# First cross-attention: denominators one step later, and every stage's first weights loaded in the stage before

## The chip, the cores and the metric

The program runs on one core of a Trainium2 chip. The metric is the device time of one execution in microseconds (us), the median of the runs of a kernel. TensorE (PE in the profile) does the matmuls and transposes, VectorE (DVE), ScalarE (ACT) and GpSimd (POOL) the rest, and SyncE (SP) issues the DMAs. Each engine works through its own stream in order and waits on semaphores for the others.

## What is computed

Four blocks follow one another on x of 4 batches x 1024 tokens x 256 channels in float32. After each of them x grows by a gate (tanh) times the block's result:

```
x = x + tanh(g_xattn[0]) * L0_xattn(layernorm(x), ctx)   # 16 heads of 16, biases, 77 keys
x = x + tanh(g_ffn[0])   * L0_ffn(layernorm(x))          # ternary weights, hidden 1024, silu/gelu
x = x + tanh(g_xattn[1]) * L1_xattn(layernorm(x), ctx)   # 8 heads of 64, own layernorm, 77 keys
x = x + tanh(g_ffn[1])   * L1_ffn(layernorm(x))          # self-attention, 8 heads, 3 of 8 chosen per token
```

In L0_xattn the head outputs are sum(exp(s) v) / sum(exp(s)). The divisor, the softmax denominator, is what the first half of the change is about.

## The kernel before, in words

There are four stages, A (`first_attention`), F (`feed_forward`), C (`cross_attention`) and E (`self_attention`). Each is a block of engine streams of its own, and between two of them all engines meet at a barrier, which also waits for the last stores. Names in the trace carry the stage's letter.

**Stage A** works on 32 tiles of 128 tokens, which make 16 pairs. Every engine runs the same loop over steps `T` from -12 to 34, with `n, odd = divmod(T, 2)`. In step T (the order is that of each stream):

- PE does the scores of tile T+2, transposes the probabilities of tile T (three groups; the first comes ahead of the next item), in an odd step transposes the widened reciprocals of pair n-1 (`reciprocals(n - 1)`, L400), in an even step transposes x of pair n+2, then in an odd step projects q of pair n+2 (L385), does half of the product with V of pair n-1 (L445), and in an even step the output projection of pair n-2 (L462).
- ACT evacuates what PE transposed, in an odd step evacuates q of pair n+2 (L528), and only then takes the exponential of tile T+2 (L564).
- POOL in `T % 8 == 0` computes the inverse roots of the next batch's layer norm (`root`, 15 small instructions), in `T % 8 == 1` their offsets, then folds the exponentials of tile T+2 into eighths (`fold`, L624, L626, L630), widens the reciprocals of tile T to one per channel (`widen`, L639), in an odd step adds the bias to x (L647), in `T % 8 == 7` spreads V into blocks (`block_v`, L659), and in the steps listed in `CHUNK_STEPS` rounds a chunk of the feed-forward's weights (L652).
- DVE takes the row maxima of tile T+2 (L754), subtracts them (L769), sums the eighths of tile T+1 and inverts (`recip_sum`, L776, L777), ors a weight chunk's bits in a `CHUNK_STEPS` step (L801), does layer-norm statistics, and in even steps weighs the attention output (L762) and adds the residual (L790).

Who waits for whom around the change:

```
reciprocals(m)  (PE)   : p_wide >= 2m + 2      # both tiles' widen
fold(T)         (POOL) : a_exp >= T + 1
widen(T)        (POOL) : d_r >= T + 1
recip_sum(T)    (DVE)  : p_eighth >= T + 1
```

**Stage F** works on 8 blocks of 512 tokens. For the first block ACT copies the transposed x out of PSUM (`xt`), copies that once more rounded (`xt_part[0]`), and POOL subtracts (`xt_part[1]`). Each block is stored with one DMA.

**Stage C** begins on SP with seven loads for weights, context and layer-norm vectors, mixed with those of x. PE's first matmuls (L1143) need Wq and the layer-norm bias.

**Stage E** begins on SP with the first slices of Wq and Wk and all of Wv. ACT, in order, rounds Wq and Wk (L2247, L2248), rounds Wv (L2376), and only then copies and rounds the four quarters of the transposed x (L2268, L2254). POOL and DVE make the low parts (L2441, L2634), and PE's first projection (L2048) needs two quarters of them.

Of the kernel before, what the change touches and what calls it, by code (L numbers as in the profile page):

```python
# [21 lines left out]
CHUNK_STEPS = (-5, -4, -2, -1, 1, 3, 4, 5, 6, 7, 9, 11, 12, 13, 15, 17, 19, 20, 21, 23, 25, 27)  # L22
# [78 lines left out]
def first_attention(nc, ident, gates, gates_src, x_src, x_dst, ctxT, wqT, wkT, wvT, woT, bias, H, ffn, head, tag):  # L101
# [43 lines left out]
    with semaphores(nc, tag) as sem, ExitStack() as ctx:  # L145
# [14 lines left out]
        ones = sb("ones", [P, P])  # L160
# [20 lines left out]
        eighth = sb("eighth", [P, 2, H, HALF // 4])  # L181
# [7 lines left out]
        w_stage = sb("w_stage", [P, STAGE, WCH])  # L189
# [41 lines left out]
        def _(sp):  # L231
# [66 lines left out]
            for dst, src in ((vbias[:, :], bv.rearrange("(c p) -> p c", p=P)),  # L298
                             (obias[:, :], spread(bo.rearrange("(a n) -> a n", a=1), 0, P))):
                sp.dma_start(dst, src, allow_slow_non_contiguous=True).then_inc(s_wide, 16)  # L300
# [301 lines left out]
        def _(pool):  # L602
# [17 lines left out]
            def fold(T):  # L620
# [7 lines left out]
                if T >= 2:  # L628
                    pool.wait_ge(d_r, T - 1)
                pool.tensor_tensor(eighth[:, T % 2, :, :], quarter[:, :, 0:HALF // 4],  # L630
# [51 lines left out]
            own.step(pool.memset(ones[:, :], 1.0))  # L682
            pool.wait_ge(s_wide, 32)
            for c in range(C):
                ins = pool.tensor_tensor(vb_wide[:, c, :], ones[:, :], spread(vbias[:, c:c + 1], 1, P), ALU.mult)
            ins.then_inc(s_vb, 1)
            pool.wait_ge(s_pad, 1)
            pool.wait_ge(root_done, 1)
            for T in STEPS:
# [7 lines left out]
                if 0 <= T < TILES:  # L697
                    widen(T)
                if odd and 0 <= n < NP:
                    add_bias(n)  # L700
                if (T + 1) % 8 == 0 and 0 <= (T + 1) // 8 < B:
                    block_v((T + 1) // 8)
                if T in CHUNK_AT:
                    round_chunk(CHUNK_AT[T])

        @block.vector
        def _(dve):
# [64 lines left out]
            def recip_sum(T):  # L772
                dve.wait_ge(p_eighth, T + 1)
                if T >= RS:
                    dve.wait_ge(p_wide, T - RS + 1)
                own.step(dve.tensor_reduce(rsum[:, T % RS, :], eighth[:, T % 2, :, :], AX.X, ALU.add))  # L776
                dve.reciprocal(rsum[:, T % RS, :], rsum[:, T % RS, :]).then_inc(d_r, 1)  # L777
# [48 lines left out]
            for T in STEPS:  # L826
# [7 lines left out]
                if 0 <= T + 1 < TILES:  # L834
                    recip_sum(T + 1)
# [7 lines left out]
                if T == -1:  # L843
                    whole_bias()
# [7 lines left out]
def cross_attention(nc, ident, gate, x_src, x_dst, ctxT, wqT, wkT, wvT, woT, bias, ln2, H, head, ahead, tag, setup=None):  # L852
# [23 lines left out]

    with semaphores(nc, tag) as sem, ExitStack() as ctx:
# [3 lines left out]
        wq_raw = sb("wq_raw", [P, DC, HD])  # L881
        wo_raw = sb("wo_raw", [P, C, D])
        wk = sb("wk", [P, DC, HD])
        wv = sb("wv", [P, DC, HD])
        cx = sb("cx", [P, 2, DC, S])
# [5 lines left out]
        ln_sb = sb("ln_sb", [P, 2, DC])  # L891
# [48 lines left out]
        s_small = sem("small")  # L940
# [20 lines left out]
        def _(sp):  # L961
# [16 lines left out]
            load_w(2, wq_raw, wqT)  # L978
            load_ctx(0)
            load_w(0, wk, wkT)  # L980
            if bias:
                bq, bk, bv, bo = bias
                for dst, src in ((qbias[:, :], bq), (kbias[:, :], bk),
                                 (vbias[:, :], spread(bv.rearrange("(a n) -> a n", a=1), 0, S)),
                                 (obias[:, :], spread(bo.rearrange("(a n) -> a n", a=1), 0, P))):
                    sp.dma_start(dst, src).then_inc(s_small, 16)
            if ln2:
                for i, v in enumerate(ln2):
                    sp.dma_start(ln_sb[:, i, :], v).then_inc(s_small, 16)
            load_w(1, wv, wvT)  # L990
            for n in range(PB):
                load_x(n)
            load_w(3, wo_raw, woT)
# [3 lines left out]
            for n in range(NP):  # L997
# [6 lines left out]
                if n:  # L1004
                    load_x(n - 1 + XR)
            for i in range(XR):
# [3 lines left out]
        def _(pe):  # L1010
            def k_proj(b):
                pe.wait_ge(s_ctx[b % 2], 16 * (b // 2) + 16)
                if b:
                    pe.wait_ge(q_made, PB * b)
# [6 lines left out]
            def v_proj(b):  # L1021
                if b == 0:
                    pe.wait_ge(s_w[1], 16)
# [25 lines left out]
            def q_proj(n):  # L1049
# [8 lines left out]
                elif n == 0:  # L1058
                    pe.wait_ge(s_w[2], 16)
# [53 lines left out]
            def out_proj(n):  # L1113
# [14 lines left out]
                elif n == 0:  # L1128
                    pe.wait_ge(s_w[3], 16)
# [8 lines left out]
            if ln2:  # L1138
                pe.wait_ge(s_small, 32)
                pe.wait_ge(s_w[2], 16)  # L1140
# [5 lines left out]
            pe.wait_ge(s_w[0], 16)  # L1146
# [27 lines left out]
        def _(act):  # L1174
# [78 lines left out]
            for T in STEPS:  # L1253
# [20 lines left out]
                if T == -2 and SPLIT:  # L1274
                    act.wait_ge(s_w[3], 16)
# [64 lines left out]
        def _(dve):  # L1340
# [89 lines left out]
            for T in STEPS:  # L1430
# [9 lines left out]
                if SPLIT and T == -12:  # L1440
                    x_low(0)
                    dve.wait_ge(s_small, 32)
                    dve.wait_ge(s_w[2], 16)
# [60 lines left out]
def feed_forward(nc, ident, gate, x_src, x_dst, fw, w, scales, s3, head, exact, tag):  # L1504
# [16 lines left out]
    with semaphores(nc, tag) as sem, ExitStack() as ctx:  # L1521
# [26 lines left out]
        e_y, d_y, rooted = sem("pe_y"), sem("y_done"), sem("root")  # L1548
        own_v, own_a, own_p = sem("own_v"), sem("own_a"), sem("own_p")
# [19 lines left out]
        def _(sp):  # L1569
            def body(b, u, i, first, last):  # L1570

                if not first:
                    sp.wait_ge(x_out[1 - u], 16 * (i + u))
                sp.dma_start(x[:, 1 - u, :, :], xd[0] if last else xs[b + 1]).then_inc(x_in[1 - u], 16)
# [1215 lines left out]
```

## Time and profile before

| what | us |
|---|---|
| median of 3 runs | 1993.03 (1991.8 to 1994.41) |
| the profiled execution | 1992.12 |
| its span, first to last instruction | 1990.4 |
| stage A, first instruction to last residual | 0 to 250 |
| stage F, from its first DMA | 254.7 to 940 |
| stage C | 944.8 to 1206.6 |
| stage E | 1210.3 to 1990.4 |

Start times in the trace are us from the span's start, so a row can be placed in its stage by this table. PE is busy 93% of the span, the next engine (DVE) 60%.

### The profile page before, as it was taken

What the parts mean: (1) busy time and instruction counts of PE and PEld (TensorE: products, weight loads), DVE (VectorE), ACT (ScalarE), POOL (GpSimd) and SP (SyncE); (2) the same over time, 40 slices, a digit from 0 to 9 for tenths busy, and PEclk for the clock granted to TensorE, in tenths of its full rate; (3) what the DMA queues carried; (4) which work ended last, traced back from release to release, by engine and by line L of the source; (5) the groups of instructions that cost most, each with busy time, mean ns of one, the idle gap of its engine ahead of it and who ended that gap; (6) DMA issues with size and microseconds to landing.
All of it is one profiled execution on the core that took longest, in us unless ns stands there. A gap on an engine that the chain in (4) does not pass through costs nothing. (4 is left out here: it accounts for less than half of the span.)

```text
span 1990.4 us, 60604 instructions
## 1 busy us (share of the span) xinstructions
PE 1845.3 (93%) x26589; PEld 1496.7 (75%) x26589; DVE 1184.3 (60%) x1654; ACT 1085.9 (55%) x1900; POOL 728.7 (37%) x1012
## 2 busy tenths in 40 slices
PE   6898779999999999998799987899999999999997
PEld 4666568787887878887678776788777887887875
DVE  7787522332323233242555543888888898888885
ACT  4666433443434344342455543677777777767763
POOL 6878601000010000000333331556655665656552
PEclk9999989999999999999799998999999999999999
DMA  5331000000000000000301004322332243223211
GB/s 178 99 101 56 23 27 1 22 21 1 22 1 22 22 1 22 0 22 12 110 28 44 30 22 118 87 66 63 93 104 58 60 109 93 61 62 109 78 51 35
DMA packets 147004, 106.23 MB, mean 53 GB/s; under 512 B 19992, under 2 KB 143152, under 8 KB 146736
## 3 DMA queue, kind: packets, MB, share of 16 engines
q1 hardware_dynamic: 146736, 102.28, 17.4%
q8 instruction: 215, 3.52, 0.7%
q14 instruction: 53, 0.43, 0.1%
HBM read 76.77 MB, written 25.49 MB: 51 GB/s over the span
## 5 line engine op out<-in xcount | busy, mean ns | idle before, releaser
L2264 ACT ACTIVATE E_prob<-E_ps_s,E_negmax 128x1024 f32<-128x1024 f32 x256 | 284.9, 1115 | 144.2 <-DVE E_negmax L2577 143.7
L2577 DVE TENSOR_REDUCE E_negmax<-E_ps_s 128x1 f32<-128x1024 f32 x256 | 301.4, 1219 | 82.6 <-PE E_ps_s L2084 82.2
L2584 DVE STREAM_TRANSPOSE E_prob<-E_prob 128x1024 f32<-128x1024 f32 x256 | 303.9, 1225 | 24.0 <-ACT E_prob L2264 11.5
L2103 PEld LDWEIGHTS E_ps_o<-E_prob,E_vrep 32*64 32x64 f32 x15872 | 231.1, 130 | 64.5 <-ACT E_part L2290 56.7
L2103 PE MATMUL E_ps_o<-E_prob,E_vrep 32*64 32x128 f32 x15872 | 262.5, 274 | 13.4 <-issue 3.9
L1690 ACT ACTIVATE F_raw<-F_ps,ffn_scales 128x512 f32<-128x512 f32 x128 | 88.3, 690 | 288.0 <-PE F_ps L1599 288.0
L1599 PE MATMUL F_ps<-F_ha,ffn_w_rounded 128*128 128x512 f32 x1024 | 240.7, 395 | 0.0
L1599 PE MATMUL F_ps<-F_hb,ffn_w_rounded 128*128 128x512 f32 x1024 | 240.2, 395 | 0.0
L1599 PEld LDWEIGHTS F_ps<-F_ha,ffn_w_rounded 128*128 128x128 f32 x1024 | 190.9, 188 | 48.4 <-issue 1.7
L1599 PEld LDWEIGHTS F_ps<-F_hb,ffn_w_rounded 128*128 128x128 f32 x1024 | 192.0, 188 | 46.9
L2480 POOL TENSOR_TENSOR E_part<-E_part 128x512 f32<-128x512 f32 x93 | 119.4, 1284 | 249.6 <-ACT E_part L2290 249.6
L1777 DVE TENSOR_TENSOR F_ha<-F_raw,F_ha 128x512 fp32r<-128x512 f32 x64 | 44.3, 692 | 184.2 <-ACT F_ha L1692 184.2
L1777 DVE TENSOR_TENSOR F_hb<-F_raw,F_hb 128x512 fp32r<-128x512 f32 x64 | 44.3, 692 | 169.2 <-ACT F_hb L1692 169.2
L1599 PE MATMUL F_ps<-F_xt_part,ffn_w_rounded 128*128 128x512 f32 x512 | 126.7, 407 | 10.7 <-POOL F_xt_part L1711 4.7
L95 POOL TENSOR_TENSOR F_rs<-F_rs 128x4 f32<-128x4 f32 x24 | 4.8, 199 | 337.5 <-DVE F_rs L1742 336.2
L2084 PE MATMUL E_ps_s<-E_k_hi,E_q_hi 64*128 64x512 f32 x512 | 114.4, 442 | 14.9 <-ACT E_prob L2264 13.5
L1599 PEld LDWEIGHTS F_ps<-F_xt_part,ffn_w_rounded 128*128 128x128 f32 x512 | 96.2, 194 | 39.0 <-DVE F_raw L1767 8.8
L1711 POOL TENSOR_TENSOR F_xt_part<-F_xt,F_xt_part 128x1024 fp32r<-128x1024 f32 x8 | 19.2, 2399 | 272.0 <-ACT F_xt_part L1658 163.9
L2084 PE MATMUL E_ps_s<-E_k_hi,E_q_lo 64*128 64x512 f32 x512 | 102.4, 393 | 0.0
L2084 PE MATMUL E_ps_s<-E_k_lo,E_q_hi 64*128 64x512 f32 x512 | 101.3, 390 | 0.0
L1767 DVE SCALAR_TENSOR_TENSOR F_raw<-F_ps,ffn_scales,F_silu 128x512 f32<-128x512 f32 x64 | 47.7, 750 | 67.7 <-ACT F_silu L1674 67.7
L2084 PEld LDWEIGHTS E_ps_s<-E_k_hi,E_q_hi 64*128 64x128 f32 x512 | 48.0, 184 | 42.6 <-ACT E_prob L2264 23.5
(315 smaller groups left out, 3912.7 us busy)
## 6 DMA issues: line engine op xcount, KB each, us to landing
E_vrep<-E_v_all SPq DMA_DIRECT2D x128, 256.0 KB, 3.0
A_w_stage<-in_L_ffn_h_wT SPq DMA_DIRECT2D x16, 512.0 KB, 3.9
E_v_all<-E_vst SPq DMA_DIRECT2D x32, 256.0 KB, 2.2
C_x<-x SPq DMA_DIRECT2D x20, 256.0 KB, 6.7
F_x<-x SPq DMA_DIRECT2D x9, 512.0 KB, 3.7
A_x<-in_x SPq DMA_DIRECT2D x16, 256.0 KB, 5.5
x<-A_x SPq DMA_DIRECT2D x16, 256.0 KB, 2.2
x<-F_x SPq DMA_DIRECT2D x8, 512.0 KB, 2.9
```

The lines of the kernel that those rows point to most:

```text
L95: own.step(eng.tensor_tensor(t, y, y, ALU.mult))
L1599: mm = pe.matmul(out, fw.chunk(w, name, k, j * P, (j + 1) * P), a[:, k, :], start=k == 0 and i == 0, stop=k == K - 1 and i == len(parts) - 1)
L1690: act.activation(raw[:, u % 2, :], ps[:, u % 4, :], ACT.Gelu, scale=scale).then_inc(u_raw, 1)
L1711: pool.tensor_tensor(xt_part[1][:, :, :], xt[:, :, :], xt_part[0][:, :, :], ALU.subtract).then_inc(xt_lo, 1)
L1767: dve.scalar_tensor_tensor(out=dst, in0=ps[:, 2 * (j % 2) + 1, :], scalar=scales[:, 1, j:j + 1], in1=silu[:, j % 2, :], op0=ALU.mult, op1= ...
L1777: dve.tensor_tensor(dst, raw[:, u % 2, :], hi, ALU.subtract).then_inc(u_lo, 1)
L2084: mm = pe.matmul(ps_s[:, j, keys], a[rows, c % 2, cols], k[rows, c % 2, keys], start=i == 0, stop=i == 2)
L2103: mm = pe.matmul(low[64 * j:64 * j + 64, g, :], vrep[rows, slot, KB // 4 * (quarter % 2) + k, dh * j:dh * (j + 1)], prob[rows, u % 2, :, j ...
L2264: act.activation(prob[:, s // UT % 2, s % UT, j, :], ps_s[:, j, :], ACT.Exp, bias=negmax[:, at:at + 1], scale=1.0, accum_out=den[:, 2 * c ...
L2480: pool.tensor_tensor(part[:, 0, :], part[:, 0, :], part[:, 1, :], ALU.add).then_inc(part_added, 1)
L2577: dve.tensor_reduce(negmax[:, at:at + 1], ps_s[:, j, :], AX.X, ALU.max, negate=True).then_inc(d_max, 1)
L2584: dve.transpose(at, at).then_inc(d_t, 1)
```

## The change

In stage A `recip_sum` of tile T moves from step T-1 to step T on DVE, and `widen` of tile T from step T to step T+1 on POOL. The eighths get a third buffer, so that `fold` may be one tile further ahead. `block_v` moves from `T % 8 == 7` to 6, `CHUNK_STEPS` is laid out anew (still 22 chunks), the whole bias is made in step 0 on DVE, and the wide bias of V is made in step -3 of POOL's loop with copies instead of ahead of the loop. PE's and ACT's streams of stage A are as before.

Stage F halves each store, loads stage C's seven first inputs during its last block into the four buffers in which stage A staged weights, and makes the first block's two parts in two halves straight from PSUM (ACT, DVE) in place of a copy. Stage C loads stage E's first three weight pieces near its end. Stage E converts its first x quarters straight from PSUM, with all low parts on DVE, ahead of the copies to `xt`, and rounds Wv later.

```diff
-CHUNK_STEPS = (-5, -4, -2, -1, 1, 3, 4, 5, 6, 7, 9, 11, 12, 13, 15, 17, 19, 20, 21, 23, 25, 27)
+CHUNK_STEPS = (-5, -4, 1, 2, 3, 4, 5, 6, 9, 10, 11, 12, 13, 14, 18, 19, 20, 21, 22, 26, 27, 28)
...
-        eighth = sb("eighth", [P, 2, H, HALF // 4])
+        eighth = sb("eighth", [P, 3, H, HALF // 4])
...
-                if T >= 2:
-                    pool.wait_ge(d_r, T - 1)
+                if T >= 3:
+                    pool.wait_ge(d_r, T - 2)
...
-            own.step(pool.memset(ones[:, :], 1.0))
-            pool.wait_ge(s_wide, 32)
-            for c in range(C):
-                ins = pool.tensor_tensor(vb_wide[:, c, :], ones[:, :], spread(vbias[:, c:c + 1], 1, P), ALU.mult)
-            ins.then_inc(s_vb, 1)
...
-                if 0 <= T < TILES:
-                    widen(T)
+                if 0 <= T - 1 < TILES:
+                    widen(T - 1)
                 if odd and 0 <= n < NP:
                     add_bias(n)
-                if (T + 1) % 8 == 0 and 0 <= (T + 1) // 8 < B:
-                    block_v((T + 1) // 8)
+                if (T + 2) % 8 == 0 and 0 <= (T + 2) // 8 < B:
+                    block_v((T + 2) // 8)
                 if T in CHUNK_AT:
                     round_chunk(CHUNK_AT[T])
+                if T == -3:
+                    pool.wait_ge(s_wide, 32)
+                    for c in range(C):
+                        ins = pool.tensor_copy(vb_wide[:, c, :], spread(vbias[:, c:c + 1], 1, P))
+                    ins.then_inc(s_vb, 1)
...
-                if 0 <= T + 1 < TILES:
-                    recip_sum(T + 1)
+                if T == 0:
+                    whole_bias()
+                if 0 <= T < TILES:
+                    recip_sum(T)
...
# stage F
                 sp.dma_start(x[:, 1 - u, :, :], xd[0] if last else xs[b + 1]).then_inc(x_in[1 - u], 16)
+                if last:
+                    for dst, src in early:
+                        sp.dma_start(dst, src).then_inc(s_early, 16)
+                sp.wait_ge(d_y, 2 * b + 1)
+                sp.dma_start(xd[b, :, 0:2, :], x[:, u, 0:2, :]).then_inc(x_out[u], 16)
                 sp.wait_ge(d_y, 2 * b + 2)
-                sp.dma_start(xd[b], x[:, u, :, :]).then_inc(x_out[u], 16)
+                sp.dma_start(xd[b, :, 2:4, :], x[:, u, 2:4, :]).then_inc(x_out[u], 16)
...
-            x_out_of_psum(0)
+            if exact:
+                act.wait_ge(e_xt, 1)
+                act.activation(xt_part[0][:, 0, :], ps_x[:, 0, :], ACT.Copy).then_inc(first_hi, 1)
+                act.activation(xt_part[0][:, 1, :], ps_x[:, 1, :], ACT.Copy).then_inc(xt_hi, 1)
...
-            x_low(0)
...
+            if exact:
+                for c in range(DC):
+                    dve.wait_ge(xt_hi if c else first_hi, 1)
+                    ins = dve.tensor_tensor(xt_part[1][:, c, :], ps_x[:, c, :], xt_part[0][:, c, :], ALU.subtract)
+                ins.then_inc(xt_lo, 1)
...
# stage C: SP loses load_w(0..3), load_ctx(0) and the two ln loads, and gains
+                if n == NP - 4:
+                    for dst, src in later:
+                        sp.dma_start(dst, src).then_inc(s_later, 16)
...
# stage E, ScalarE
             split_weights(0)
-            act.wait_ge(wv_in, 16)
-            act.activation(wv[0][:, :, :], wv_raw[:, :, :], ACT.Copy).then_inc(wv_hi, 1)
             for q in range(NQ):
                 act.wait_ge(done["x"], q + 1)
+                act.activation(xt_part[0][:, :, q * PAIR:(q + 1) * PAIR], banks[4 + q].rearrange("p (k w) -> p k w", k=DC),
+                               ACT.Copy).then_inc(c_hi, 1)
+            for q in range(NQ):
+                act.wait_ge(c_lo0, q + 1)
                 x_out(q, banks[4 + q].rearrange("p (i w) -> p i w", w=TOK)).then_inc(free["x"], 1)
-                convert(q, q)
             first_qk("k", 0, banks[0])
             first_qk("q", 0, banks[1])
             first_qk("k", 1, banks[2])
+            act.activation(wv[0][:, :, :], wv_raw[:, :, :], ACT.Copy).then_inc(wv_hi, 1)
```

## Rows read from the trace of the kernel before

**Rows 1.** The page's busy time by engine, us, share and instructions
```profile
PE 1845.3 (93%) x26589; PEld 1496.7 (75%) x26589; DVE 1184.3 (60%) x1654; ACT 1085.9 (55%) x1900; POOL 728.7 (37%) x1012
```
**Rows 2.** Windows in stage A: length, busy by engine, clock, DMA
```profile
124.95:136.37 11.42, 11.34 (x114) 8.07 (x111) 10.17 (x15) 7.88 (x15) 8.86 (x12) 1.00 0.60 188
142.24:159.82 17.58, 13.05 (x111) 8.87 (x110) 9.15 (x11) 9.14 (x17) 15.87 (x36) 0.90 0.18 61
```
**Rows 3.** Timeline of stage A, a batch boundary on DVE and PE
```profile
152.46 0.32 DVE L776 TENSOR_REDUCE A_rsum<-A_eighth 128x16 f32<-128x160 f32 x1 [6.43 <-POOL A_eighth L630]
154.84 1.75 PE L445 MATMUL A_ps_o<-A_pt,A_v_blk 128*32 128x256 f32 x16 [4.45 <-issue]
```
**Rows 4.** Timeline of stage A, the reciprocals' transposes on PE and one exponential
```profile
132.05 0.60 PE L400 MATMUL A_ps_m<-ident,A_r_wide 128*128 128x128 f32 x4
...
141.29 1.23 ACT L564 ACTIVATE A_prob<-A_prob 128x1232 f32<-128x1232 f32 x1 [1.63 <-DVE A_prob L769]
...
228.29 0.63 PE L400 MATMUL A_ps_m<-ident,A_r_wide 128*128 128x128 f32 x4 [1.25 <-DVE A_x L790]
```
**Rows 5.** Timeline of stage A, POOL through steps 13 to 16
```profile
126.09 1.52 POOL L624 TENSOR_TENSOR A_half_sum<-A_prob 128x624 f32<-128x624 f32 x1 [2.87 <-ACT A_prob L564]
...
130.77 1.03 POOL L652 CAST ffn_w_rounded<-A_w_stage 128x1024 fp32r<-128x1024 f32 x1
...
131.77 1.52 POOL L624 TENSOR_TENSOR A_half_sum<-A_prob 128x624 f32<-128x624 f32 x1
...
134.75 0.52 POOL L639 COPY A_r_wide<-A_rsum 128x128 f32<-128x128 f32 x2
...
137.52 1.53 POOL L624 TENSOR_TENSOR A_half_sum<-A_prob 128x624 f32<-128x624 f32 x1 [2.25 <-ACT A_prob L564]
...
144.98 0.24 POOL L609 TENSOR_SCALAR A_rs<-A_mv 128x8 f32<-128x8 f32 x1
...
149.41 1.52 POOL L624 TENSOR_TENSOR A_half_sum<-A_prob 128x624 f32<-128x624 f32 x1
```
**Rows 6.** Timeline of stage A, the first batch on POOL and PE
```profile
30.22 1.53 POOL L624 TENSOR_TENSOR A_half_sum<-A_prob 128x624 f32<-128x624 f32 x1 [1.07 <-ACT A_prob L564]
...
48.11 0.81 PE L414 MATMUL A_ps_s<-A_kt,A_q 32*128 32x154 f32 x16 [1.98 <-DVE A_prob L769]
...
49.41 1.06 PE L400 MATMUL A_ps_m<-ident,A_r_wide 128*128 128x128 f32 x4
...
56.07 1.51 POOL L624 TENSOR_TENSOR A_half_sum<-A_prob 128x624 f32<-128x624 f32 x1 [1.71 <-ACT A_prob L564]
```
**Rows 7.** Timeline of stage A, a fold beside a DVE instruction on weight bits
```profile
117.16 1.73 DVE L801 TENSOR_TENSOR A_w_bits<-A_w_bits,A_w_stage 128x1024 int32<-128x1024 int32 x1
...
118.07 2.19 POOL L624 TENSOR_TENSOR A_half_sum<-A_prob 128x624 f32<-128x624 f32 x1 [0.26 <-ACT A_prob L564]
```
**Rows 8.** Timeline of stage F's start
```profile
256.86 1.02 ACT L1656 ACTIVATE F_xt<-F_ps_x 128x1024 f32<-128x1024 f32 x1 [10.49 <-PE F_ps_x L1588]
...
259.05 2.34 POOL L1711 TENSOR_TENSOR F_xt_part<-F_xt,F_xt_part 128x1024 fp32r<-128x1024 f32 x1 [19.84 <-ACT F_xt_part L1658]
```
**Rows 9.** Timeline of stage C's start
```profile
947.87 1.12 PE L1046 MATMUL C_ps_m<-ident,head 128*128 128x128 f32 x4 [9.07 <-issue]
...
953.79 3.57 PE L1143 MATMUL C_ps_o<-C_ln_sb,C_wq_raw 128*128 128x1 f32 x16 [4.81 <-DMA C_ln_sb<-in_L_xattn_ln_bias]
```
**Rows 10.** Timeline of stage E's start
```profile
1210.30 3.35 PE L2033 MATMUL E_ps_s<-ident,ahead 128*128 128x128 f32 x16 [4.47 <-PEq L37]
...
1218.96 0.71 DVE L2634 TENSOR_TENSOR E_xt_lo<-E_xt,E_xt_hi 128x512 fp32r<-128x512 f32 x1 [12.35 <-ACT E_xt_hi L2254]
...
1219.82 0.76 PE L2048 MATMUL E_ps_o<-E_xt_hi,E_wk_hi 128*128 128x512 f32 x1 [6.17 <-DVE E_xt_lo L2634]
```
**Rows 11.** DMA issues of the page: KB each, us to landing
```profile
x<-A_x SPq DMA_DIRECT2D x16, 256.0 KB, 2.2
x<-F_x SPq DMA_DIRECT2D x8, 512.0 KB, 2.9
```

More of the change, by code:

```diff
@@ L775, in recip_sum @@
                     dve.wait_ge(p_wide, T - RS + 1)
-                own.step(dve.tensor_reduce(rsum[:, T % RS, :], eighth[:, T % 2, :, :], AX.X, ALU.add))
+                own.step(dve.tensor_reduce(rsum[:, T % RS, :], eighth[:, T % 3, :, :], AX.X, ALU.add))
                 dve.reciprocal(rsum[:, T % RS, :], rsum[:, T % RS, :]).then_inc(d_r, 1)
@@ L849, in _, with cross_attention @@
             dve.wait_ge(d_inexact, 1)
-def cross_attention(nc, ident, gate, x_src, x_dst, ctxT, wqT, wkT, wvT, woT, bias, ln2, H, head, ahead, tag, setup=None):
+def cross_attention(nc, ident, gate, x_src, x_dst, ctxT, wqT, wkT, wvT, woT, bias, ln2, H, head, early, ahead, later, tag, setup=None):
     B, _, S = ctxT.shape
@@ L1580, in _ @@
             for u in range(XR):
-                sp.wait_ge(x_out[u], 16 * (NB // XR))
+                sp.wait_ge(x_out[u], 32 * (NB // XR))
+            sp.wait_ge(s_early, 16 * len(early))
         @block.tensor
@@ L1883, in self_attention @@
         wwide = sb("wwide", [P, UT, P])
-        part = sb("part", [P, 2, 512])
+        part = spare[:, :, :].rearrange("p (a b) d -> p a (b d)", a=2)
         wrow = sb("wrow", [P, 512])
@@ L2241, in split_weights @@
             def split_weights(n):
[L2243 removed]
+                if n:
+                    act.wait_ge(w_in, 32 * n)
                 if n == 1:
@@ L2513, in _ @@
             split_weights(0)
-            for q in (0, 2):
-                convert(q, q)
             pool.wait_ge(wv_hi, 1)
@@ L2725, in gated_layers @@
         head = ctx.enter_context(nc.sbuf_tensor("head", [P, 4, D], F32))
+        shared = ctx.enter_context(nc.sbuf_tensor("shared", [P, STAGE, WCH], F32))
+        c_ctx = ctx.enter_context(nc.sbuf_tensor("c_ctx", [P, 2, DC, t["ctxT"].shape[2]], F32))
+        c_ln = ctx.enter_context(nc.sbuf_tensor("c_ln", [P, 2, DC], F32))
+        HD, rows = t["L1_xattn_Wq"].shape[1], "(c p) n -> p c n"
+        c_wq, c_wk, c_wv = (shared[:, i, :].rearrange("p (c n) -> p c n", n=HD) for i in range(3))
+        c_wo = shared[:, 3, :].rearrange("p (c n) -> p c n", n=D)
+        early = ((c_wq, t["L1_xattn_Wq"].rearrange(rows, p=P)),
+                 (c_ln[:, 0, :], t["L1_xattn_ln_scale"]), (c_ln[:, 1, :], t["L1_xattn_ln_bias"]),
+                 (c_ctx[:, 0, :, :], t["ctxT"][0].rearrange(rows, p=P)),
+                 (c_wk, t["L1_xattn_Wk"].rearrange(rows, p=P)), (c_wv, t["L1_xattn_Wv"].rearrange(rows, p=P)),
+                 (c_wo, t["L1_xattn_Wo"].rearrange(rows, p=P)))
         with ExitStack() as ffn_ctx:
```

102 lines of the change are left out of this document (36 added, 66 removed).

## The prediction

> **What bounds the kernel now.** I read the page first: PE is busy 93% of the span [rows 1], so only places where PE waits can give or take much. The change touches four of them: the inside of stage A and the starts of F, C and E. Then I put windows on stage A. Between batch boundaries a pair of steps takes 11.42 us, and PE is busy for 11.34 of them [rows 2]: PE is the bound there. The pair that holds a boundary takes 17.58 us. The timeline says why: POOL does its 15 small root instructions, so the fold behind them is late, DVE stands 6.43 us at the sum of the eighths, and PE, which needs DVE's next weighing, waits 4.45 us [rows 3]. This is the stall at which the later denominators aim. It occurs three times.
>
> **What the later widening does to PE.** Let R be the start of PE's transposes of the reciprocals in an odd step T. It needs widen(T-2). Before, POOL does this in its step T-2; after, in step T-1, behind fold(T+1). Take pair 6 (T = 15): R is 132.05 [rows 4]. Fold(16) began at 131.77, and what was widened behind it ran from 134.75 to 135.27 [rows 5]. In the place that the change gives it, the widening is 3.2 us late for PE. The question is whether POOL can get ahead. It can't, for this is a loop through both engines, with these terms:
>
> - From R to the next fold in the odd step: 5.47 (132.05 to 137.52). In between lie PE's other transposes, the q projection and ACT's q evacuation, behind which stands the exponential that ends POOL's wait of 2.25 [rows 4, 5].
> - From that fold through widening, bias and cast to the next fold: 5.68 (126.09 to 131.77), or 4.68 where the step has no cast (to 130.77) [rows 5].
> - That fold and the widening behind it: 3.50 (131.77 to 135.27), and 0.05, my guess for the signal to PE.
>
> The sum is 14.70 for a pair of steps with a cast in the odd one, where PE alone needs 11.42. Without the cast it would be 13.70, but the even step's exponential, ended at 142.52 (141.29 and 1.23) [rows 4], lets that fold start 10.47 after R at the earliest, not 10.15, which makes 14.0. At a boundary the root stands ahead of the fold, between the last two terms: 4.43 (144.98 to 149.41) [rows 5], so 18.13. The spreading of V and the cast of step 7 leave this place, which is right for the DVE stall (it goes, as recip_sum has one more fold in hand), but the wait is now PE's, in the middle of its stream, and q, the exponentials and the folds are all queued behind it.
>
> **Stage A summed.** The first R. Before, a spreading of V and a cast stood between fold(1) and the root; now they are gone or earlier. Fold(1) starts at 30.2 as before and takes 3.05, the root 4.43, so fold(2) starts at 37.7; with 3.05, and 0.65 for two offset instructions (like the root's, some 0.3 each), fold(3) starts at 41.4, fold(4) at 47.1, and R follows at 50.7 against 49.41 [rows 6]: what the start had won, the size of a cast and a spreading, is already spent. From the first pair's R to that of the fourteenth (T = 29, 228.29 before [rows 4]) there are 13 loops: 8 with a cast in the odd step (3, 5, 9, 11, 13, 19, 21, 27), 2 without, 3 with a root. 8 x 14.70 + 2 x 14.0 + 3 x 18.13 = 200.0, so R of pair 13 is at 250.7, 22.4 later than before. After it no q is projected and the tail is as it was.
>
> **The clock.** Each loop leaves PE idle for about 3 us. In the boundary pair the granted clock is 0.90 over 17.58 us [rows 2], which is some 3.5 us at 1.2 in place of 2.4 GHz, behind the wait of 4.45 [rows 3]. Behind a wait of only 1.98, in the first batch, R's transposes took 1.06 in place of 0.60, and the next fold came 6.66 after R (49.41 to 56.07) in place of 5.47 [rows 6]: 1.19 on this very path. Behind a wait of 1.25 they took 0.63, the full clock's time [rows 4]. A wait of 3 lies between two that were followed by the lower clock, so I take each loop to begin at 1.2 GHz. Over 13 loops 15.5 us. The bounds are 0 and 15.5; I take 15.5. Stage A: +22.4 + 15.5 = +37.9. The Trainium skill (TensorE: Matmul & The Clock Gate, Loop structure matters more than you think) says the same of loops: whether matmuls stay warm is settled by the loop nest, and a wait in every pass leaves them cold. By that page the 15.5 stand; if the clock stayed up they would be nothing.
>
> **POOL beside DVE.** POOL is in the loop now, so what lengthens it counts. A fold took 2.19 in place of 1.52 beside DVE's instruction on weight bits, which itself took 1.73 [rows 7]. Eleven even steps have a chunk, whose bits DVE ors at about the time of the even fold: 11 x 0.67 = 7.4 us at most. DVE has slack now and can lie elsewhere; I take 0 and keep 7.4 for the range. The Trainium skill (GPSIMD Engine Reference, Specifications) says GpSimd shares its SBUF interfaces with VectorE and contends with instructions of two SBUF inputs, as this one is. The row agrees; by the page the sum would be nearer its upper bound.
>
> **F's start.** Before: ACT from 256.86, twice over the whole, then POOL 2.34, done at 261.39 [rows 8]. After: two halves of ACT's 1.02, 0.6 each with what an instruction costs by itself, and DVE's 0.71 more (the size of E's low part [rows 10]): 256.86 + 1.20 + 0.71 + 0.1 = 258.9. Gain 2.5.
>
> **F's end.** The last store has 256 KB, which land in 2.2, not 2.9 [rows 11]: gain 0.7. SP issues the seven early loads at the last block's start, some 70 us ahead of its next store; they are hidden by F's matmuls, which read no DRAM, and would cost at most SP's issue of them.
>
> **C's start.** PE's second group begins at 953.79 after a wait of 4.81 for the layer-norm bias; the loads now lie behind, so it begins at 948.99: gain 4.8. DVE's parts of Wq, four instructions of twice 0.71 at most behind 949.6, are done by 955.3, and the q projection comes only behind two groups of 16 matmuls, 3.57 the first and as much again the second at this clock, 956.1. That PE begins only at 947.87, 3.1 after SP, with its idle time put down to issue, I leave as it is; the bounds are 0 and a gain of 3.1 [rows 9].
>
> **E's start.** The transposes end at 1213.65. Wq and Wk are in SBUF, so ACT rounds them as the stage begins, and POOL's low parts, half the 2.34 of rows 8 for half the size, are ready by 1213. Two quarters are ready at about 1213.4: the second group of transposes ends at 1212.0, then ACT's 0.6 and DVE's 0.71. The first projection starts at 1213.7, not 1219.82 [rows 10]: gain 6.1. If PE keeps 2.4 GHz as its wait is gone, the 12 matmuls of the first two projections save up to 1.8 more (0.76 the first, at the low clock, and about 0.4 less for each pair); I take 0.9. Wv's rounding lies in a stretch in which ACT waits for the first maxima, and POOL's low part of it ends about when PE wants it: nothing, or 0.5. E's body is PE's own and moves as a whole.
>
> **The sum.** 37.9 - 2.5 - 0.7 - 4.8 - 7.0 = +22.9. On the profiled execution's 1992.12 this makes 2015.0; the median of the runs lies 0.9 above it, so I say 2015.5.
>
> **The rivals.**
> (a) The loop is there but the clock stays up: +22.9 - 15.5 = +7.4, 2000. For it: the waits of 3 us are not those of 4.45. Against: 1.98 was enough. Chance 0.20.
> (b) The loop, the low clock, and POOL beside DVE at its full price: 2022.9. Chance 0.08.
> (c) Faster: the widening is ready when PE comes. Then the three boundary pairs fall from 17.58 to about 11.42, 2.7 are won at the start and 15.0 at the starts of F, C and E: -36, 1957. It decides at one point: fold(T+1) must begin at least 3.55 us before R. The rows have it 0.28 before (131.77 and 132.05), and the cast and bias ahead of it make up only 2.3 of the 3.3 that lack. Only if POOL's or ACT's order were not what the loop needs would it hold. Chance 0.12, a part of it for values between, down from -6.
> (d) The gains at the stage starts and the loss in A cancel: within 4 us of 1993 (0.2% is about what a measurement of this kernel can tell). It needs a loop of some 13 us at full clock. Chance 0.03.
> My forecast has 0.57. Slower 0.85, same 0.03, faster 0.12. The range leaves out (c) and (d) and ends a little beyond (b): 1996 to 2024.
>
> **What the profile would show.** Right: PE's row L400 waits for POOL L639, some 3 us in nearly every odd step and 6 to 7 at the three boundaries; the distance between L400 rows is near 16 (14.7 if the clock is up); DVE's wait at L776 is gone; stage A ends near 288; the gap before L1143 is gone and that before L2048 is under 1. Wrong: L400 rows still 11.4 apart, or POOL idle and ahead of R. The forecast is wrong as a whole if R's condition is met by work in another order than I read.

## The result and the profile after

The changed kernel takes 2035.65 us (median of 4 runs, 2032.69 to 2037.14) against 1992.41 us of the kernel before on the same chip: 1.0221 times as long, with a 95% interval of 1.0206 to 1.0236. That is some 43 us more. The prediction said slower, and named the mechanism, but with +22.9: 2015.5 in a range of 1996 to 2024. The time lies outside the range.

The page's busy line of the changed kernel answers to [rows 1]. PE does the same instructions in 45 us more, and is busy for 11.6 us of them:

```profile
PE 1856.9 (91%) x26589; PEld 1509.1 (74%) x26589; DVE 1188.2 (58%) x1658; ACT 1086.3 (53%) x1900; POOL 731.2 (36%) x1008
```

**Where the time went.** I cut both traces at the last residual of A (DVE, 249.58 before and 309.38 after), the last DVE instruction of F (939.56, 993.58) and of C (1205.86, 1251.77), and the end of PE's last matmul (1986.14, 2031.16). Stage A: +59.8. F: -5.8. C: -8.1. E: -0.9. The sum is +45.0, the difference of the two spans. So in these two traces the three starts together gave 14.8 where 15.0 were forecast, and the miss is in stage A: +59.8 where 37.9 were forecast.

**The wait in stage A.** These are PE's transposes of the reciprocals (now L398) from the timeline of the changed kernel, one in an ordinary pair and two behind boundaries; they answer to [rows 4, 6]:

```profile
144.15 0.66 PE L398 MATMUL A_ps_m<-ident,A_r_wide 128*128 128x128 f32 x4 [1.51 <-POOL A_r_wide L637]
...
180.09 1.12 PE L398 MATMUL A_ps_m<-ident,A_r_wide 128*128 128x128 f32 x4 [6.64 <-POOL A_r_wide L637]
...
251.56 1.12 PE L398 MATMUL A_ps_m<-ident,A_r_wide 128*128 128x128 f32 x4 [6.63 <-POOL A_r_wide L637]
```

All 14 such rows up to 287.36 end a wait for POOL's widening (L637), 9.27 us the first, 6.6 to 7.4 at the boundaries and 1.19 to 5.0 in the other pairs, 64.1 us in all. In the kernel before 12 of these 14 show no wait. From 144.15 to 180.09 lie two pairs, 15.66 and 20.28 us, as the windows of the changed kernel show beside [rows 2] (length, busy by engine, granted clock, DMA):

```profile
144.15:159.81 15.66, 11.47 (x111) 8.07 (x111) 14.08 (x29) 7.98 (x14) 10.81 (x14) 0.94 0.58 164
159.81:180.09 20.28, 13.65 (x110) 10.07 (x110) 8.29 (x12) 8.09 (x14) 13.71 (x33) 0.84 0.17 53
```

PE's busy time in a pair is what it was, 11.4, where it keeps its clock; the rest is idle. DVE's wait for the eighths at a boundary [rows 3] is gone, as the change does what it says; a stall stands on PE instead, in every pair, and at a boundary it is longer than PE's 4.45 there before.

**The three parts of the loop.** The prediction took the loop apart at R (the start of those transposes), the odd fold and the even fold. Summed over the 13 loops of a trace, in us:

| kernel | first R | R to odd fold | to even fold | to next R | 13 loops | A's last residual | time |
|---|---|---|---|---|---|---|---|
| before | 49.41 | 87.9 | 95.0 | -4.0 | 178.9 | 249.6 | 1992.4 |
| forecast | 50.7 | 86.6 | 82.7 | 46.2 | 215.5 | 287.5 | 2015.5 |
| changed | 53.39 | 91.5 | 90.7 | 51.8 | 234.0 | 309.4 | 2035.65 |

(A negative number: the even fold begins behind the next R, so PE does not wait for it.) The forecast's row is its own arithmetic: 13 x 6.66; 8 x 5.68 and 2 x 4.98 and 3 x 9.11; 13 x 3.55. Each of the three parts was longer than forecast, by 4.9, 8.0 and 5.6, and the first R was 2.7 later.

**POOL's part.** The two POOL parts name their cause in the timeline. POOL's widening and DVE's instruction on the weight bits (L799), behind the odd fold at 149.62 of the changed kernel:

```profile
152.53 0.25 DVE L775 RECIPROCAL A_rsum<-A_rsum 128x16 f32<-128x16 f32 x1
152.70 1.26 DVE L799 TENSOR_TENSOR A_w_bits<-A_w_bits,shared 128x1024 int32<-128x1024 int32 x1
...
152.59 1.52 POOL L637 COPY A_r_wide<-A_rsum 128x128 f32<-128x128 f32 x2
...
159.23 0.53 POOL L637 COPY A_r_wide<-A_rsum 128x128 f32<-128x128 f32 x2
```

The widening is two copies of 0.29 us. Beside L799 it takes 1.52 to 1.61, and in a step without weight bits 0.53. In the changed kernel this is no chance meeting: DVE ends its sum and POOL its fold at about the same moment, and on DVE the bits, on POOL the widening, come next. In the groups by form, from 53 to 288 us on POOL, the widening is 461 ns a copy, where it was 294 in the loops of before:

```profile
L637 POOL COPY A_r_wide<-A_rsum 128x128 f32<-128x128 f32 x54 | 23.3, 461 | 0.0
```

The new steps of the casts have a part in this: in the run below with the late denominators and the old steps, 2 widenings take 1.5 us or more, here 9.

L799 hits other POOL instructions too. In the first batch a root instruction of 0.25 us whose record begins 0.02 before L799's ends 0.09 behind it, and two sums are 0.9 and 1.0 too long. Together this is 2.8, about the 2.7 by which the first R is late:

```profile
37.26 1.27 POOL L97 TENSOR_SCALAR A_rs<-A_rs 128x8 f32<-128x8 f32 x1
...
43.98 1.72 POOL L624 TENSOR_TENSOR A_quarter<-A_half_sum 128x320 f32<-128x320 f32 x1
...
48.90 2.48 POOL L622 TENSOR_TENSOR A_half_sum<-A_prob 128x624 f32<-128x624 f32 x1
...
37.28 1.16 DVE L799 TENSOR_TENSOR A_w_bits<-A_w_bits,shared 128x1024 int32<-128x1024 int32 x1
```

**The clock.** Behind a wait of 1.2 to 1.5 the way from R to the odd fold is 5.48 (three pairs), the forecast's full-clock figure. Behind 4 us and more it is 6.8 to 7.9, not 6.66. The windows of the changed kernel behind the wait of 4.19 that ends at 198.03 show why: the granted clock is 0.50 (1.2 GHz) until past 202, so it lies over the transposes and most of the q projection (200.22 to 203.15).

```profile
198.00:200.00 2.00, 1.97 (x9) 1.97 (x10) 0.00 (x0) 0.60 (x1) 0.96 (x1) 0.50 0.06 6
200.00:202.00 2.00, 2.00 (x7) 1.64 (x7) 0.00 (x0) 0.87 (x2) 0.00 (x0) 0.50 0.76 256
202.00:204.00 2.00, 2.00 (x21) 1.06 (x19) 0.00 (x0) 0.81 (x3) 0.00 (x0) 0.92 0.00 0
```

**The starts.** PE's first matmuls on loaded data in F, C and E of the changed kernel, for [rows 8 to 10]:

```profile
318.73 1.62 PE L1578 MATMUL F_ps<-F_xt_part,ffn_w_rounded 128*128 128x512 f32 x3 [2.10 <-DVE F_xt_part L1746]
...
1001.36 1.11 PE L1028 MATMUL C_ps_m<-ident,head 128*128 128x128 f32 x4 [8.55 <-issue]
1002.27 3.41 PE L1119 MATMUL C_ps_o<-c_ln,shared 128*128 128x1 f32 x16
...
1256.26 3.64 PE L2019 MATMUL E_ps_s<-ident,ahead 128*128 128x128 f32 x16 [4.53 <-PEq L37]
1259.70 0.76 PE L2034 MATMUL E_ps_o<-E_xt_hi,E_wk_hi 128*128 128x512 f32 x1
```

From A's last residual to F's first product it is 9.35 us, 11.95 before: 2.6 won, 2.5 forecast. In C the wait of 4.81 is gone. In E the first projection comes 3.44 behind the first transposes, 9.52 before: 6.1 won, and the first scores 7.4 (9.61 and 17.00), where 7.0 was forecast.

### The profile page after: what moved, and what is told of

Read it like the earlier page. It is cut to its first block and busy times, and to the rows that moved or that the text cites. A ratio compares the mean times of both kernels' runs of the same rounds, so it can differ in the third digit from the quotient of the medians.

```text
span 2035.4 us, 60621 instructions
## 1 busy us (share of the span) xinstructions
PE 1856.9 (91%) x26589; PEld 1509.1 (74%) x26589; DVE 1188.2 (58%) x1658; ACT 1086.3 (53%) x1900; POOL 731.2 (36%) x1008
## 5 line engine op out<-in xcount | busy, mean ns | idle before, releaser
L2571 DVE STREAM_TRANSPOSE E_prob<-E_prob 128x1024 f32<-128x1024 f32 x256 | 304.0, 1226 | 23.8 <-ACT E_prob L2251 11.4
L2469 POOL TENSOR_TENSOR head<-head 128x512 f32<-128x512 f32 x93 | 119.0, 1279 | 254.4 <-ACT head L2277 254.4
L622 POOL TENSOR_TENSOR A_half_sum<-A_prob 128x624 f32<-128x624 f32 x32 | 51.9, 1623 | 83.3 <-ACT A_prob L562 83.0
```

The lines of the kernel that those rows point to most:

```text
L622: own.step(pool.tensor_tensor(half_sum[:, :, 0:S2 // 2], prob[:, T % PR, :, 0:S2 // 2], prob[:, T % PR, :, S2 // 2:S2], ALU.add))
L2469: pool.tensor_tensor(part[:, 0, :], part[:, 0, :], part[:, 1, :], ALU.add).then_inc(part_added, 1)
L2571: dve.transpose(at, at).then_inc(d_t, 1)
```

## The experiments

Theory 1 is the prediction's own: the widening of tile T, put behind the fold of tile T+3, closes a loop through PE, ACT and POOL, and this lengthens stage A. What the loop costs over the forecast is then POOL beside DVE and the clock. The rivals: the new steps of the casts and of V's spreading are to blame, or the clock alone is.

### Denominators as before, the rest changed

```
-                if 0 <= T - 1 < TILES:
-                    widen(T - 1)
+                if 0 <= T < TILES:
+                    widen(T)
...
-                if T == 0:
-                    whole_bias()
-                if 0 <= T < TILES:
-                    recip_sum(T)
+                if 0 <= T + 1 < TILES:
+                    recip_sum(T + 1)
```

(`eighth` has two buffers again, and the whole bias is made in step -1.)

> The changed kernel with the denominators of stage A summed and widened where they were before; the new steps of the casts and of the spreading of V, and all the early loads, stay. Theory 1 (the widening behind the next fold makes a loop through POOL and PE, and this alone lengthens stage A): stage A returns to its length of before, within 5 us, and the three starts keep what they gained (some 15 us in the traces: F 6, C 7, E 1 to 2): about 1978. Rival theory (the new steps of casts, bits and spreading collide with the folds and cost most of the 60 us): stage A stays 30 us or more longer, and the time is over 2010.

1971.13 us, 0.9898 of the kernel before (0.9873 to 0.9922). Stage A ends at 243.55, 6 us before that of the kernel before, and the wait for the widening is gone: PE's waits at R are for DVE's residual, 1.5 at most. F is 685.4 long, C 258.4, from the same cuts. Theory 1 stands for the 60 us, and the rival falls: by themselves the new places of casts and spreading don't cost, they gain. A boundary pair takes 13.9 to 14.7 us with them, not 17.58, though DVE still waits 3.81 for the eighths there (6.43 in [rows 3]):

```profile
153.21 0.63 PE L398 MATMUL A_ps_m<-ident,A_r_wide 128*128 128x128 f32 x4 [1.50 <-DVE A_x L788]
...
145.71 0.32 DVE L774 TENSOR_REDUCE A_rsum<-A_eighth 128x16 f32<-128x160 f32 x1 [3.81 <-POOL A_eighth L628]
```

### The late denominators alone

The same edit the other way round, in the kernel before.

> The kernel before with the later sums and the later widening alone. Theory 1: stage A is some 60 us longer and nothing else moves, so about 2052; the distance of the reciprocals' transposes in a pair is near 16 or more. Rival theory: with the old steps of casts and spreading the later denominators cost at most some 25 us, 2015 or less.

2053.48 us, 1.0323 (1.0298 to 1.0349). Stage A ends at 310.91, +61.3, and nothing else gains. With spreading and cast back in step 7 the boundary is worse: the wait is 10.29 and the loop 23.2.

```profile
255.08 1.12 PE L400 MATMUL A_ps_m<-ident,A_r_wide 128*128 128x128 f32 x4 [10.29 <-POOL A_r_wide L639]
```

The two runs together part the change: the late denominators cost some 64 us (2035.65 against 1971.13, and 2053.48 against 1990.03, its own comparison), everything else gives some 18 to 19.

### The widening ahead of root and fold

```
             for T in STEPS:
                 n, odd = divmod(T, 2)
+                if 0 <= T - 1 < TILES:
+                    widen(T - 1)
                 if T % 8 == 0 and 1 <= (T + 8) // 8 <= B:
                     root((T + 8) // 8)
...
-                if 0 <= T - 1 < TILES:
-                    widen(T - 1)
```

> The changed kernel with POOL's widening of tile T-1 put at the head of step T, ahead of the root and of the fold of tile T+2. Theory 1: the loop is then 5.47 + (5.68 - 0.52) + 0.57 = 11.2 us, just under PE's own 11.4, so PE no longer waits at the reciprocals; the boundary pairs fall from 17.6 to about 11.4 to 13 as DVE's stall is gone too; stage A some 15 to 21 us shorter than before, the starts 15 shorter, so 1956 to 1965. If the cause lies in the casts and their contention, it stays over 2000.

1969.19 us, 0.9895 (0.9873 to 0.9918); a second time, below, 1969.61. The denominators stay late; only the place in POOL's stream differs from the changed kernel, and 66 us go. The loops fall from 234.0 to 172.6. I had expected 1956 to 1965. What lacks can be read from the loops: ordinary pairs take 11.4 to 12.3, but the pair behind a boundary still waits, 4.90 for the first and 1.8 for the others, and POOL works through nearly all of it (busy 11.89 of 13.36 us, the last of the five busy times, behind 10.84 of 11.40 in the pair ahead of it):

```profile
134.74:146.14 11.40, 11.28 (x110) 8.12 (x111) 9.49 (x21) 7.39 (x13) 10.84 (x20) 1.00 0.43 140
146.14:159.50 13.36, 11.52 (x112) 8.00 (x110) 11.73 (x13) 8.47 (x15) 11.89 (x27) 1.00 0.18 60
```

The forecast of 11.2 for this loop left contention out: the cast takes 2.03 to 2.04 in place of 1.03 beside L799.

### PE's wait filled

```
             def reciprocals(n):
-                pe.wait_ge(p_wide, 2 * n + 2)
                 if n:
                     pe.wait_ge(d_fin, n)
                 else:
                     pe.wait_ge(x_taken, 4)
+                if n <= NP - 3:
+                    for _ in range(16):
+                        pe.transpose(ps_m[:, 0:P], ident[:, :], ident[:, :])
+                pe.wait_ge(p_wide, 2 * n + 2)
```

> The changed kernel with 16 idle transposes of the identity (128x128, about 0.15 us each at full clock, 2.4 us in all) into the PSUM bank that the reciprocals' transposes write next, just ahead of their wait, in the 14 pairs of the loop. The widening comes no earlier, so by itself it can win nothing; if the low clock behind each wait costs what the trace suggests (about 2.2 us on the way from the reciprocals to the next fold, in about nine loops, plus other work), stage A falls by 15 to 25 us and the time is 2012 to 2020. If the clock doesn't matter, or the fills are too short to keep it up, 2035 or a little more.

2029.81 us, 1.0204 (1.0179 to 1.0229): some 6 us less, under the 15 to 23 that the expectation asked of a clock effect. The parts say that 16 were too few: R to odd fold fell from 91.5 to 84.6, and at the boundaries PE still waited 4.9 to 5.9. So I filled more, 44 in the first and the boundary pairs, 10 in pairs 1, 5 and 9, else 28:

> As the kernel with 16 idle transposes, but as many as fill most of each wait: 44 in the first and the boundary pairs, 10 in the pairs whose wait is short, 28 in the others. With 16 the transposes of the reciprocals kept the full clock in most pairs but the stretch behind them did not. If the low clock follows the idle time of PE, the way from the reciprocals to the next fold comes near 5.47 in all 13 loops (91.5 us in the changed kernel, 71 at full clock), and the time is 20 us less than the changed kernel's 2035, so about 2015, with a few us given back where the fills are longer than the wait. If the fills don't matter beyond what 16 did: about 2029.

2019.53 us, 1.0144 (1.0127 to 1.016), 16 us less than the changed kernel. R to odd fold is 72.2 (12 loops of 5.47 or 5.48), the two POOL parts are unchanged (91.6 and 51.1), and stage A ends at 288.66, 20.7 earlier. The same pairs at the granted clock 1.00, and one of the fills:

```profile
136.99:152.69 15.70, 14.53 (x138) 11.13 (x139) 14.10 (x29) 7.98 (x14) 10.84 (x14) 1.00 0.55 142
152.69:170.92 18.23, 16.27 (x154) 12.88 (x155) 8.25 (x12) 7.98 (x14) 13.70 (x33) 1.00 0.24 80
```
```profile
164.12 4.97 PE L395 MATMUL A_ps_m<-ident 128*128 128x128 f32 x44
170.92 0.66 PE L401 MATMUL A_ps_m<-ident,A_r_wide 128*128 128x128 f32 x4 [1.83 <-POOL A_r_wide L640]
```

PE does useless work here and the stage is shorter for it: the low clock cost the changed kernel 91.5 - 72.2 = 19.3 us of the loop. Stage C is some 4 us longer in the three kernels with fills than in most other changed ones (262 to 263 against 258), which is why the whole gained less. The clock is part of it: at C's start V's projection takes 2.82 to 3.39 there and 1.88 in most others. It is not the fills alone, since a run without them (the bits in the odd steps, below) has 2.77 and a C of 260.4, and the kernel before has 2.66.

### DVE's bits cut to 8 columns

```
-                    dve.tensor_tensor(w_bits[:, :], w_bits[:, :], words, ALU.bitwise_or).then_inc(d_bits, 1)
+                    dve.tensor_tensor(w_bits[:, 0:8], w_bits[:, 0:8], words[:, 0:8], ALU.bitwise_or).then_inc(d_bits, 1)
```

(This kernel leaves out the search of the other 1016 columns of a chunk, so it only measures what the long instruction costs.)

> The changed kernel, but DVE's instruction on the weight bits ors 8 columns of a chunk and not all 1024, so the search for inexact weights is incomplete in it. In the trace of the changed kernel POOL's widening takes 1.5 to 1.6 us in place of 0.52 wherever this DVE instruction lies beside it, and some folds 2.2 in place of 1.5. Theory 1 (POOL is in the loop, so these lengthen stage A): the two POOL terms of the 13 loops, 90.7 and 51.8 us, fall to about 83 and 46, stage A is 13 us shorter, and some 2022. Rival (the clock alone makes what was left over): nothing, 2035, since POOL waits for the exponentials in any case.

2015.27 us, 1.0121 (1.0104 to 1.0138), 20 us less. The widening is back at 0.53 with the short DVE instruction beside it:

```profile
142.84 0.53 POOL L637 COPY A_r_wide<-A_rsum 128x128 f32<-128x128 f32 x2
...
142.95 0.20 DVE L799 TENSOR_TENSOR A_w_bits<-A_w_bits,shared 128x8 int32<-128x8 int32 x1
```

First R 49.73; the parts 85.6, 83.6 and 46.5; 215.7 for the 13 loops; stage A ends at 287.39. The forecast had 86.6, 82.7, 46.2, 215.5 and 287.5. With DVE's long instruction out of the way the sums of the parts are those that I predicted, within 1 us. In the first part this is luck: I had 6.66 in each of the 13 loops, and the run has 5.47 or 5.48 in four of them and 6.56 to 7.68 in the others. The time, 2015.27 against 2015.5, has the same luck in it. It gained more than the 13 us expected because the first R comes 3.7 earlier (2.8 of it are the three instructions above, the rest lies ahead of the first folds) and because the first part is 5.9 shorter. That POOL's own instructions became shorter, and not only DVE's load, is in POOL's busy time: 731.2 in the changed kernel, 715.0 here, and the first R and the two POOL parts together give the same 16.1.

### Both

The fills of the second kind and the 8 columns.

> The two together: DVE ors 8 columns only (the search for inexact weights is incomplete), and PE's waits are filled with idle transposes. This is the loop as the prediction summed it, at full clock and without contention: 14.70 with a cast, 14.0 without, 18.13 with a root, 200 us from the first reciprocals to the fourteenth (234 in the changed kernel), and 34 us less than the changed kernel as a whole, about 2001. If a term of the loop was mis-sized by itself, the distances stay longer than these though clock and contention are gone.

2005.89 us, 1.0078 (1.0057 to 1.01); expected 2001. Pairs with a cast take 14.66 (forecast 14.70), boundary pairs 18.26 to 18.28 (18.13):

```profile
129.59:144.25 14.66, 14.48 (x140) 11.07 (x139) 11.76 (x21) 7.99 (x14) 9.77 (x14) 1.00 0.63 172
144.25:162.51 18.26, 16.27 (x154) 12.87 (x154) 9.21 (x20) 7.99 (x14) 13.74 (x33) 1.00 0.20 70
```

The 13 loops take 206.6, not 200.0. In two loops the low clock is there in spite of the fills: the first (17.09) and one behind a boundary (16.15) take 7.16 and 7.14 from R to the odd fold, which is 3.4 of the 6.6. The rest lies mostly in the other pairs behind the boundaries (14.5 to 15.2), where the forecast had 14.0 to 14.7.

The four kernels make a square. Cutting the bits gives 20.4 without the fills and 13.6 with them, so some 7 of its 20 come by way of the clock; the fills give 16.1 with all bits and 9.4 with few.

### Root behind the fold

In the kernel with the widening first, `root` stands behind `fold(T + 2)`.

> The kernel with the widening first, and POOL's root of a boundary step put behind the fold of that step in place of ahead of it. The fold, and with it the denominators, come 4.4 us earlier at each boundary; the layer norms that need the root come 3 us later and have slack. Theory 1: the waits for the widening at the pair behind a boundary (4.9, 1.8, 1.8 us) and POOL's lateness go, 3 to 8 us less than with the widening first alone: 1961 to 1966. Rival (POOL is the bound in that pair in any order): the same time, 1969.

1974.77 us, 0.9918 (0.9901 to 0.9935): no gain, perhaps a loss. The loops take 174.4 and the pair behind a boundary 13.41 as before it. The rival holds: in that pair POOL's instructions follow one another without a wait in either order (busy 11.71 of 13.41 here), so POOL is the bound there.

### The bits in the odd steps

```
-                if T in CHUNK_AT:
-                    mantissas(CHUNK_AT[T])
+                if odd:
+                    for U in (T - 1, T):
+                        if U in CHUNK_AT:
+                            mantissas(CHUNK_AT[U])
```

> The kernel with the widening first, and DVE's instruction on the weight bits of an even step done in the odd step behind it, where POOL waits some 2.9 us for the odd exponential. In the trace with the widening first a POOL instruction that meets this DVE instruction takes about 1 us more (the cast 2.03 in place of 1.03, the widening 1.52 in place of 0.53, the quarter sum 1.73 in place of 0.87), ten times or so in the pairs. Theory 1: the waits for the widening that are left (0.7 us in most pairs, 4.9 and 1.8 at the boundaries) shrink, and it is 3 to 8 us below the kernel with the widening first. Rival (DVE, full in these pairs, weighs later for it and PE waits for the residual): equal or some 3 us slower.

> The kernel with the widening first once more, on the same chip, for the comparison: 1969, 21 us below the kernel before; the trace as in its first run, but PE's idle time that no wait explains in stage E may differ by some 3 us.

1971.58 (0.9901, 0.9881 to 0.992) and, for the comparison, 1969.61 (0.9902, 0.9885 to 0.9919): nothing. The place was right, for the ordinary pairs fell from 12.28 to 11.47, and the 13 loops from 172.1 to 169.6. The end gave it back. DVE then does bits, last search and weighing in one step, PE waits, and the low clock follows; the timeline of this kernel on PE:

```profile
227.12 2.78 PE L443 MATMUL A_ps_o<-A_pt,A_v_blk 128*32 128x256 f32 x18 [3.03 <-DVE A_o L760]
229.83 3.32 PE L460 MATMUL A_ps_m<-A_wo,A_o 128*128 128x256 f32 x8
```

With the last chunk's bits left in their even step:

> As the kernel with the bits in the odd steps, but the last chunk's bits stay in their even step, ahead of the last search. In the trace of the kernel with all bits in odd steps the full pairs fell from 12.28 to 11.47 us, but DVE did the last bits (1.46) and the last search (1.41 and 1.22) in one step, PE waited 3.03 for the weighing behind them and went on at the low clock (2.78 and 3.32 for two groups that take 1.5 and 1.99 at the full one), so the step from the fourteenth to the fifteenth reciprocals took 14.44 in place of 9.5. Theory 1: this one keeps the first and not the second, stage A ends near 241, and it is 3 to 5 us below the kernel with the widening first: 1964 to 1967. Rival: what the pairs win is lost in the start and at the boundaries again, 1969.

1968.25 us, 0.9901 (0.9884 to 0.9917). Stage A ends at 240.38, the earliest of all (242.53 and 244.42 with the widening first alone), but the whole can't be told from 1969. Three kernels of about 1970, some 20 us under the kernel before, are the best found: denominators as before, widening first, and this one.

## Why the prediction was right and where it was wrong

- **The loop.** Right in mechanism and nearly in size. At the full clock and without contention the pairs are 14.66 and 18.26 where 14.70 and 18.13 were summed; pairs behind a boundary are up to 0.5 longer than summed. In the run with 8 columns stage A ends 0.1 us from the forecast, in part by luck, as said there. That the late denominators are the cause is shown from both sides (1971 without them, 2053 with them alone), and that it is the place behind the fold and not the lateness is shown by the widening put first (1969).
- **POOL beside DVE: the step that failed.** The prediction wrote "DVE has slack now and can lie elsewhere; I take 0" and had 11 x 0.67 = 7.4 as the most, and it put the case at 0.08. Cutting DVE's instruction took 20 us off the time, 22 off stage A: 3.7 before the first R, 7.1 and 5.3 in the two POOL parts, 5.9 in the part of the clock. What was wrong is the count and the price. I priced a fold that meets L801 and began ahead of its end [rows 7], but didn't ask what POOL does at the moment at which the moved DVE instruction would begin: it is mostly the widening, behind the odd fold seven times and behind the even one twice, and it loses 1.0 and not 0.67 (an even fold that meets L799 still loses 0.67: 2.19 at 139.94). The Trainium skill (SBUF — State Buffer, section "SBUF: two separate sides") calls the port pair that DVE and GpSimd share "an exclusive lock, not a bandwidth split". This case agrees: the root instruction of 37.26 ends at 38.53, just behind L799's end at 38.44, though its record begins 0.02 ahead. By that rule a short POOL instruction can lose the whole length of L799, 1.16, however short it is, and a bound of 0.67 was never one. Priced at 1.0 for each of the 22 chunks the upper bound would have been 22; 16 came so, and 6 more by way of the clock. With 22 in place of 7.4 the sum reaches 2037.5.
- **The clock.** Right that every long wait (4 us and more) is followed by 1.2 GHz, mis-sized. I had 1.19 a loop from a row behind a wait of 1.98 [rows 6], 15.5 in all. The runs show 91.5 - 72.2 = 19.3: nothing in the three loops behind waits of 1.2 to 1.5, 1.3 to 2.4 in the others. About 6 of this come only with the longer waits that the contention makes.
- **The first R.** 50.7 forecast, 53.39 measured, 49.73 with 8 columns: again the contention.
- **F's start and end.** 2.5 and 0.7 forecast. The first product is 2.6 earlier. The end's gain lies behind the cut, in C: SP's first instruction is 4.4 behind F's last one on DVE, where it was 5.2, so 0.8. By the cuts F itself is 5.8 shorter in this trace and 4.6 to 5.6 in those of the runs above with the changed F (7.9 in one). Only 2.6 of it are explained. A part is that F's length differs between traces: the run with the late denominators alone has F as before and 688.1 us, 1.9 less than the 690.0 before.
- **C's start.** 4.8 forecast, 8.1 by the cuts, with the 0.8 of F's store in it. The first scores of C come 16.7 behind SP's first instruction, where it was 22.1: 5.4. Another 0.8 is V's projection, which takes 1.88, before 2.66, by the clock. This is not the change's doing: the run with the late denominators alone, whose C is that of before, has 1.88 too, and its C is 263.7 long and not 266.3. That PE begins some 3 behind SP is as before (3.1 and 3.4).
- **E's start.** 7.0 forecast, 7.4 at the first scores, and only 0.9 at the end. Of it 2 are given back by 1310: PE waits longer for ACT's exponentials (1.92 in place of 0.37) and goes on at the low clock (3.72 for a group that took 2.09). The step "E's body is PE's own and moves as a whole" failed. The remaining difference lies mostly in PE's idle time that no wait explains, 12.8 us in this trace against 9.3 before. In the ten other traces with this E it was 8.4 to 13.8, and E's length mostly went with it (775.1 at 8.4, 775.3 at 9.2, 779.2 at 12.0, 779.9 at 13.8, but 776.2 at 13.1). Against the 780.3 of the kernel before, at 9.3, the gain is 5. Where that idle time comes from stays open.
- **The sum of the starts.** 15.0 forecast, 14.8 measured, and this is luck: C and F show more than forecast and E less. Against the trace with the late denominators alone, which has F, C and E as before, the three are 3.9, 5.5 and 2.0, together 11.4.
- **The last step of the sum.** 22.9 on the median of the kernel before, 1993.03, is 2015.9, not 2015.5; it changes nothing.
- **The rivals.** (c), faster with the widening ready in time, was the right picture of another order: its 1957 is what the widening first aimed at, and reached 1969 for POOL's work behind the boundaries. (b) came nearest, with a price of 7.4 where 16 to 22 came.

## What to carry to other kernels

When an instruction is moved a step later on its engine, ask what it then stands behind, not only when its input is there: here one fold of 3 us ahead of a 0.5 us copy made a loop through three engines and cost some 60 us, with the contention and the low clock that it brought, and putting the copy first took it all back. Contention that costs nothing while an engine has slack is paid in full once that engine is in the loop: POOL's busy time was 728.7 us before and 731.2 in the changed kernel, so its instructions had met DVE's long one before as well, and only then did it count (715.0 with that instruction cut). And once an engine is in a loop with PE, price its contention and PE's clock per pass from the worst row, not from the nearest.

## What the runs showed of the hardware

- A short POOL instruction that meets DVE's instruction on the bits ends just behind it: at 38.53 and 38.44, 154.11 and 153.96, 197.98 and 197.83. One that begins 0.1 earlier goes free and DVE's waits the 0.1: at 103.90 a root instruction of 0.20 is not held, and of the two copies that begin at 119.09 only the second is (from 119.32, 1.29 in place of 0.29), with 1.27 for L799 in place of 1.16.
- It goes both ways. In the first run with the widening first the bias of 130.92 ends at 132.20, L799 of 131.11 ends at 133.28 (2.17 in place of 1.16), and the cast of 132.14 ends at 134.18 (2.04 in place of 1.03): each ends about 1 us behind the end of the one before it.
- The low clock can begin behind the wait, when PE is already at work again. In the run with the late denominators alone a wait of 3.10 ended at 128.31; the windows show 1.00 through the wait, 0.99 in the 1.7 us behind it, and only then 0.50:

```profile
125.00:128.30 3.30, 0.21 (x2) 0.00 (x0) 3.23 (x5) 0.60 (x1) 3.10 (x5) 1.00 0.79 226
128.30:130.00 1.70, 1.56 (x11) 1.36 (x12) 1.03 (x1) 0.99 (x3) 0.00 (x0) 0.99 0.44 178
130.00:132.00 2.00, 2.00 (x6) 1.56 (x6) 0.00 (x0) 0.37 (x2) 0.00 (x0) 0.50 0.00 0
132.00:134.00 2.00, 2.00 (x20) 0.93 (x18) 0.00 (x0) 0.66 (x2) 0.00 (x0) 0.66 0.00 0
```

  So transposes at the full clock's 0.66 behind a wait do not tell that the clock stayed up: the next fold came 7.07 behind them, not 5.47. Nor does the length of the wait alone tell it: in the run with 8 columns one of 2.10 that ends at 184.76 is followed by 6.57 to the fold, one of 2.11 that ends at 250.18 by 5.47.
- Idle transposes in a wait pay: 44 of them in 4.97 us stood in a boundary pair whose granted clock was 1.00, and the stage was 20.7 us shorter with the fills. Where 16 stood in each wait, it was 6.4 us shorter.
